# A decoder block with top-2 experts: the routing joined to the gating's program, with other prefix sums and 16-bit one-hot products

## What is computed

```python
def _L0_ffn_ref(x, gate_w, expert_w):                     # x = ln(x), 8 experts, 1024 x 1024 each
    gate_logits = jnp.einsum('bsh,he->bse', x, gate_w)
    top_vals, top_idx = jax.lax.top_k(gate_logits, 2)
    probs = jax.nn.softmax(top_vals, axis=-1)
    w_e = jnp.einsum('bsk,bske->bse', probs, jax.nn.one_hot(top_idx, 8))
    expert_out = jnp.einsum('bsh,eho->bseo', x, expert_w)
    return jnp.einsum('bseo,bse->bso', expert_out, w_e)
```

## Time and profile before

| what | us |
|---|---|
| median of 3 runs | 1199.26 |
| lowest and highest | 1190.36, 1199.87 |
| the profiled execution | 1194.41 |
| its span in the trace | 1192.4 |
| PE, DVE, POOL, ACT busy in it | 1042.3, 570.3, 487.3, 393.8 |

### The profile page before, as it was taken

How to read it: one execution, slowest core, us unless ns; L and a number is a source line. 1 busy time by engine, 2 the same in 40 slices (tenths; PEclk the granted TensorE clock), 3 DMA queues, 4 the chain that set the end, 5 groups by cost and what they waited for, 6 DMA issues and landing times. The chain is left out here.

```text
span 1192.4 us, 13599 instructions
## 1 busy us (share of the span) xinstructions
PE 1042.3 (87%) x3593; PEld 575.2 (48%) x3594; DVE 570.3 (48%) x1637; ACT 393.8 (33%) x1124; POOL 487.3 (41%) x661
## 2 busy tenths in 40 slices
PE   6786888888888869989965699999999999999995
PEld 6784454454544435425965344444444444444442
DVE  5636479788888677996965211111111111211111
ACT  2435778676756316866830000000000000000000
POOL 3834467546655201005710643333444333334431
PEclk9878899888889979988765799999999999999998
DMA  8310110110000123000795247354645636374432
GB/s 304 121 54 0 46 68 13 54 36 1 1 1 1 70 79 134 1 1 18 283 350 215 73 86 226 74 177 104 211 79 136 169 73 211 70 211 82 86 78 36
DMA packets 38462, 120.27 MB, mean 101 GB/s; under 512 B 6219, under 2 KB 9350, under 8 KB 38406
## 3 DMA queue, kind: packets, MB, share of 16 engines
q1 hardware_dynamic: 25590, 79.77, 18.1%
q0 software_dynamic: 12816, 39.86, 15.4%
HBM read 82.91 MB, written 36.70 MB: 100 GB/s over the span
## 5 line engine op out<-in xcount | busy, mean ns | idle before, releaser
L1952 PE MATMUL bank<-T,X 128*128 x1184 | 510.6, 594 | 13.9 <-DVE X L1990 10.8
L1952 PEld LDWEIGHTS bank<-T,X 128*128 128x128 f32 x1184 | 225.2, 191 | 298.6 <-issue 298.6
L2004 DVE TENSOR_SCALAR X<-bank,col_p 128x512 f32<-128x512 f32 x37 | 27.8, 750 | 410.5 <-PE bank L1952 410.5
L1970 ACT ACTIVATE X<-bank,col_p 128x512 f32<-128x512 f32 x37 | 25.4, 687 | 523.2 <-PE bank L1952 523.2
L1905 POOL DMA_INDIRECT X<-x_nrm,col_s x156 | 149.5, 958 | 92.9 <-issue 46.9
L1914 POOL DMA_INDIRECT out_dram<-X,col_d x37 | 60.0, 1622 | 268.6 <-DVE X L2004 255.0
L450 POOL TENSOR_TENSOR T<-T 128x8 f32<-128x8 f32 x216 | 94.5, 437 | 16.3
L634 PE MATMUL bank<-nat,T 128*128 128x512 f32 x128 | 88.0, 840 | 12.1 <-ACT X L787 5.4
L799 ACT ACTIVATE M<-X,T 128x256 bf16<-128x256 f32 x200 | 98.5, 497 | 0.0
L459 POOL TENSOR_TENSOR rs<-ve,neg_half 128x4 f32<-128x4 f32 x36 | 38.5, 1069 | 104.7 <-DVE ve L942 104.5
L787 ACT ACTIVATE X<-bank,T 128x512 f32<-128x512 f32 x64 | 43.8, 686 | 70.1 <-PE bank L634 69.6
(11 more groups left out here) (317 smaller groups left out, 1462.9 us busy)
## 6 DMA issues: line engine op xcount, KB each, us to landing
T<-in_L_ffn_expert_w_dram SPq DMA_DIRECT2D x8, 4096.0 KB, 17.6
out_dram<-X SPq DMA_DIRECT2D x17, 512.0 KB, 4.7
M<-in_x_dram SPq DMA_DIRECT2D x16, 512.0 KB, 7.3
X<-in_x_dram SPq DMA_DIRECT2D x16, 512.0 KB, 4.7
x_nrm<-H SPq DMA_DIRECT2D x16, 512.0 KB, 3.7
T<-in_ctx_dram SPq DMA_DIRECT2D x9, 512.0 KB, 4.0
X<-x_nrm,col_s POOLq DMA_INDIRECT x156, 3.6
X<-in_ctx_dram SPq DMA_DIRECT2D x4, 512.0 KB, 7.0
```

The lines of the kernel that those rows point to most:

```text
L1952: mm = nc.tensor.matmul(bank[2 * u + n][:, :], xgt[u][:, k, :], Tf[:, ds(odd * (KD * D) + (k * D + n * BANK), BANK)], start=(k == 0), stop ...
```

## The change

The routing's block is gone: its instructions stand at the end of the gating's block, and its small tiles are declared ahead of it. In the routing the prefix sums over tiles come from one scan by DVE on the choices themselves, and PE adds the column sums and a triangle with -1 at and below the diagonal in PSUM, so that several small DVE steps fall away. The one-hot lanes and slots are bf16: a token's number is split into two parts that bf16 holds exactly, and a weight into three pieces. The products of the weights, and what says which slot has which expert, are moved behind the first `sources` of the experts' block, beside the gathers. Expert 0 is loaded in the middle of the gating. The second part of tile 12 goes ahead of the last `back`, batch 0 takes its statistics ahead of `first_sums`, and the last steps of the logits change order. Row numbers count from 1, which costs one more row of `x_nrm`, and T's two halves for the weights are interleaved.

```diff
@@ gating, SP @@
+                    if b == B // 2:
+                        sp.wait_ge(back_mm, 2 * B)
+                        sp.wait_ge(l_mm, NT // 2)
+                        sp.dma_start(wslot[:, 0, :, :], expert_src(0)).then_inc(w_in_sem[0], 16)
                 sp.dma_start(out[N:N + P, :], X[:, 0, :]).then_inc(out_init, 16)
+                sp.dma_start(x_nrm[0:1, :], nring[0][0:1, :]).then_inc(out_init, 16)
                 sp.wait_ge(back_mm, 4 * B)
-                sp.wait_ge(l_mm, B)
-                for w in range(2):
-                    sp.dma_start(wslot[:, w, :, :], expert_src(w)).then_inc(w_in_sem[w], 16)
+                sp.wait_ge(l_mm, NT)
+                sp.dma_start(wslot[:, 1, :, :], expert_src(1)).then_inc(w_in_sem[1], 16)
@@ gating, PE @@
+                    upto = CT * b if b < B - 2 else CT * b + 1 if b < B - 1 else CT * B
+                    for t in range(done, upto):
+                        second_part(t)
...
+                pe.wait_ge(r_dve, 14)
+                nc.tensor.matmul(bank[TOTAL][:, 0:E], ones[:, :], prefix[:, :, NT - 1], start=True, stop=True).then_inc(r_pe, 1)
+                nc.tensor.matmul(bank[PLACE][:, 0:NT * E], upto_neg[:, :], flat(either), start=True, stop=False)
+                nc.tensor.matmul(bank[PLACE][:, 0:NT * E], ones[:, :], flat(prefix), start=False, stop=True).then_inc(r_pe, 1)
+                for k in range(2):
+                    pe.wait_ge(hot_set, k + 1)
+                    for t in range(NT):
+                        mm = nc.tensor.matmul(bank[TOKEN][:, 0:2 * WIDE], hot_lane[k][:, t, :], of_token[k][:, t, :, :]...)
+                for c in range(QK):
+                    for j in range(2):
+                        mm = nc.tensor.matmul(bank[SOURCE][...], sel[:, c, :], tok_parts[:, j, 0:SLOTS], ...)
@@ gating, ACT @@
+                for k in range(QK):
+                    a.copy(sel[:, k, :]..., ident[:, k * QP:(k + 1) * QP]...).then_inc(r_sel, 1)
+                a.copy(lane_row, iota_lane[:, :]).then_inc(r_sel, 1)
+                a.activation(tile_base, step_t[:, 0, :]..., ACT.Copy, scale=float(QK)).then_inc(r_sel, 1)
                 for h in range(CT):
                     normed((B - 1) * CT + h)
+                act.wait_ge(r_dve, 13)
+                a.activation(e2[:, :], e2[:, :], ACT.Exp).then_inc(r_act, 1)
@@ gating, DVE @@
                 for b in range(B):
                     residual(b)
+                    if b > 0:
+                        behind(b - 1)
+                    stats(b)
                     if b == 0:
                         first_sums(2)
                         first_sums(3)
-                    else:
-                        behind(b - 1)
-                    stats(b)
...
-                behind(B - 1)
+                dve.wait_ge(l_mm, NT)
+                then(v.tensor_tensor(known, known, bank[P2_BANK]..., ALU.add))
                 then(v.tensor_tensor(shift, over_e(mean_all(1)), over_t(g_all), ALU.mult))
                 then(v.tensor_tensor(known, known, shift, ALU.subtract))
-                dve.wait_ge(l_mm, B)
-                then(v.tensor_tensor(known, known, bank[P2_BANK]..., ALU.add))
+                behind(B - 1)
                 then(v.tensor_tensor(logits[:, :, :], known, over_e(rs_all(1)), ALU.mult))
...
+                route(v.tensor_tensor_scan(prefix..., later_t[:, :], either..., 0.0, ALU.mult, ALU.add))
+                dve.wait_ge(r_pe, 1)
+                route(v.tensor_tensor(full, step_t, bank[TOTAL]..., ALU.is_lt))
+                route(v.tensor_reduce(need, full, AX.X, ALU.add))
+                route(v.tensor_tensor_scan(end, ones[:, 0:E], need, 0.0, ALU.mult, ALU.add))
+                dve.wait_ge(r_pe, 2)
+                route(v.scalar_tensor_tensor(place, begin..., float(P), bank[PLACE]..., ALU.mult, ALU.add))
+                route(v.tensor_tensor(hot[:, :, :, :], hot[:, :, :, :], place..., ALU.mult))
+                route(v.tensor_reduce(pos_i[:, :, :], hot[:, :, :, :], AX.X, ALU.add))
+                v.tensor_scalar(lane_i, pos_i, P - 1, None, ALU.bitwise_and)
+                route(v.tensor_scalar(slot_i, pos_i, 7, None, ALU.logical_shift_right))
+                dve.wait_ge(r_sel, QK + 2)
+                v.tensor_copy(lane[:, :, :], lane_i[:, :, :])
+                for k in range(2):
+                    route(v.tensor_tensor(at_slot[k]..., iota_slot..., slot_i[:, k, :]..., ALU.is_equal))
+                    v.tensor_scalar(of_token[k][:, :, 0, 0:SLOTS], at_slot[k]..., tok1[:, 0:1], float(QK), ALU.mult, ALU.mult)
+                    v.tensor_tensor(of_token[k][:, :, 1, 0:SLOTS], at_slot[k]..., tile_base..., ALU.mult)
+                    for t in range(NT):
+                        ins = v.tensor_scalar(hot_lane[k][:, t, :], lane_row, lane[:, k, t:t + 1], None, ALU.is_equal)
+                    ins.then_inc(hot_set, 1)
+                dve.wait_ge(r_act, 1)
...
+                weigh(dve, v.tensor_copy(piece[0], prob[:, :, :]))
+                weigh(dve, v.tensor_tensor(prob_rest[0], prob[:, :, :], piece[0], ALU.subtract))
...
+                dve.wait_ge(r_pe, 3)
+                v.tensor_copy(tok_parts..., bank[TOKEN]...).then_inc(tok_set, 1)
+                for j in range(2):
+                    weighted(0, j)
+                dve.wait_ge(r_pe, 4)
+                route(v.tensor_scalar(src_i..., bank[SOURCE]..., quarter[:, 0:1], None, ALU.add))
@@ experts, SP @@
+                sp.wait_ge(cols_set, IN_FLIGHT)
@@ experts, POOL @@
-                pool.wait_ge(out_init, NT * 16 + 16)
+                pool.wait_ge(out_init, NT * 16 + 32)
@@ experts, PE, ahead of the first products @@
+                for k in range(2):
+                    pe.wait_ge(p_set, k + 1)
+                    for t in range(NT):
+                        mm = nc.tensor.matmul(bank[PROB][:, 0:3 * WIDE], hot_lane[k][:, t, :], of_prob[k][:, t, :, :]...)
+                mm.then_inc(p_mm, 1)
@@ experts, DVE @@
                 for u in range(IN_FLIGHT):
                     sources(u, u)
-                    columns(u, u)
+                weighted(0, 2).then_inc(p_set, 1)
+                v.tensor_scalar(end_i[:, :], end, 1.0, None, ALU.add)
+                weigh(dve, v.tensor_tensor(past, iota_slot..., end..., ALU.is_ge))
...
+                for j in range(3):
+                    ins = weighted(1, j)
+                ins.then_inc(p_set, 1)
+                turned(0, 0, 0)
+                sources(IN_FLIGHT, 0)
...
+                dve.wait_ge(p_mm, 1)
+                weigh(dve, v.tensor_reduce(pair_p[:, :], bank[PROB]..., AX.X, ALU.add))
+                for u in range(IN_FLIGHT):
+                    columns(u, u)
```

More of the change, by code:

```diff
@@ new lines, in decoder_kernel @@
+        best = small(2, NT)
+        hot = small(2, NT, E)
+        eq = small(NT, E)
+        first = small(NT)
+        masked = small(NT, E)
+        either = small(E, NT)
+        e2 = small(NT)
+        prob = small(2, NT)
+        prefix = small(E, NT)
+        full = small(E, NT)
+        need = small(E)
+        ends = small(E + 1)
+        begin, end = ends[:, 0:E], ends[:, 1:E + 1]
+        place = small(NT, E)
+        pos_i = small(2, NT, dt=I32)
+        lane_i = small(2, NT, dt=I32)
@@ new lines, in decoder_kernel @@
+        lane_row = small16(P)
+        tile_base = small16(NT, WIDE)
+        sel = small16(QK, QK * QP)
+        hot_lane = [natf[:, k * N:k * N + NT * P // 2].bitcast(BF16).rearrange("p (t l) -> p t l", t=NT) for k in range(2)]
+        at_slot = [small16(NT, WIDE) for _ in range(2)]
+        of_token = [small16(NT, 2, WIDE) for _ in range(2)]
+        of_prob = [small16(NT, 3, WIDE) for _ in range(2)]
+        piece = [small16(2, NT) for _ in range(3)]
+        prob_rest = [small(2, NT) for _ in range(2)]
@@ new lines, in decoder_kernel, with weigh, weighted @@
+        tok_parts = small16(2, WIDE)
+        tok4 = small(SLOTS)
+        pair_p = small(SLOTS)
+        unused = small(SLOTS)
+        src_i = small(SLOTS, QK, dt=U32)
+        p_set, p_mm, r_fin = sem("p_set"), sem("p_mm"), sem("r_fin")
+        n_weigh = [0]
+        def weigh(dve, ins):
+            n_weigh[0] += 1
+            ins.then_inc(r_fin, 1)
+            dve.wait_ge(r_fin, n_weigh[0])
+        def weighted(k, j):
+            return nc.vector.tensor_tensor(of_prob[k][:, :, j, 0:SLOTS], at_slot[k][:, :, 0:SLOTS], piece[j][:, k, :].unsqueeze(2).to_broadcast([P, NT, SLOTS]), ALU.mult)
@@ L1713, in decoder_kernel @@
-        best = small(2, NT)
-        hot = small(2, NT, E)
-        eq = small(NT, E)
-        first = small(NT)
-        masked = small(NT, E)
-        either = small(NT, E)
-        e2 = small(NT)
-        prob = small(2, NT)
-        tot = small(E, NT)
-        upto = small(E, NT)
-        full = small(E, NT)
-        need = small(E)
-        end = small(E)
-        begin = small(E)
-        place = small(NT, E)
-        pos = small(2, NT)
-        pos_i = small(2, NT, dt=I32)
-        lane_i = small(2, NT, dt=I32)
```

(26 more changed lines are left out.)

254 lines of the change are left out of this document (122 added, 132 removed).

## The result

Over 20 executions each, the changed kernel has a median of 1187.97 us and the kernel before one of 1199.37 on the same chip. Two of the changed kernel's 20 took 1400.27 and 1563.72 us, at a mean granted clock of 0.715 and 0.633 for 0.90 in the others, and the ratio leaves them out. It is 0.9924, with a 95% interval of 0.9905 to 0.9943: 0.8% faster, some 9 us by the means (11 by the medians). I had forecast 23 less and a range that ended at 1184.

The account below looks back on a forecast made before the run. What can move lies ahead of the experts' fixed PE-busy stage: 4.95 (boundary) + 1.3 (gating) + 17.0 (routing) + 0.3 (sources) - 0.5 (first gather) = 23 us less than a base of 1197, so 1174 us; range 1164 to 1184.

Parts of the forecast that it names:

- What binds: Experts' stage fixed at 513.8 us; every microsecond taken ahead of it, from gating to first gathers, ends up in the time.
- The gating: Stage up to the logits: ready 1.3 us earlier, at 613.9; bounds from a 0.8 us loss to 3 us gained.
- (a): Gating: batch 0's statistics fill DVE's 2.71 us wait for PE, moving PE's gapless stretch to the logits forward by 2.1 us.
- (b): Gating: second part of tile 12 ahead of the last `back`, same number of PE passes; no gain.
- (c): Gating's end: DVE's steps after the last product take 1.5 us instead of 0.72, a loss of 0.8 us.
- The boundary: Between gating and routing: without a block between, DVE goes on after the logits; all 4.95 us go.
- The routing: From the logits to `src_i`: 18.1 us for 35.15, 17.0 less; bounds 15.5 to 25.5 us.
- The tail: Routing's end, behind PE's token products up to `src_i`: 2.2 us, where now it is 3.7.
- Behind the boundary: Start of experts: sources done 0.3 us earlier; moved DVE and PE work hidden beside the gathers, 1.3 us of cover left.
- The rival: DVE's four two-source products beside descriptor writing delay the first gather by up to 3.2 us: 1177 us; chance 0.14.
- ACT and DMA: Early expert 0 load delays stores, still done before the gathers ask; expert 1's load can cost the first gather 0.5 us.
- the rival of the choked queue: Early expert load delays the stores the gathers wait for: 1180 us at 250 GB/s, 1199 at worst; chance 0.07.

Follow-up runs that it names:

- the run with one compare: Changed kernel with batch 0's statistics behind the first sums again and each choice's sixteen compares made in one instruction: 1178.3 us, ratio 0.9845 to the kernel before.
- the change with the wait: Changed kernel with PE waiting for three quarters of batch 3's residual, not one, ahead of batch 4's turning back: 1176.9 us, ratio 0.9839 (first job 1178.6).
- the longer one: Changed kernel with PE waiting for all four quarters of batch 3's residual ahead of batch 4's turning back: 1180.8 and 1185.2 us, ratio 0.9891.

## Why the prediction was wrong, point by point

**What binds** held: the experts' stage kept its length, and what was gained ahead came through. The base of 1197 was a choice between two values; the mean of the kernel before over its 20 executions is 1197.2, their median 1199.4, so the miss isn't there.

**The gating is the step that failed.** Its part (a) had DVE's lead move PE's stretch "forward by 2.1 us" at the length it had. It moved by 1.24 (31.00 for 32.24 us), since DVE lost 1.8 us of the 2.7 again: two shifts of 128 x 1, 0.68 us at that place before, took 2.46 beside POOL's product, and the next two gave 0.3 back. That alone is a small error. The large one is the length: I moved the stretch as it stood, with 168 ns for each of its last 64 passes, as if that were the price of a pass, when it was the price at the clock that this kernel happened to get. At 1.2 GHz the 160 passes of 8 columns and the 64 of 128 make 47.50 us, at the mixture 35.09. The windows that I had read said 0.78 for that stretch and 0.50 for what came after; my bound for the loss was 0.8 us, and nothing in the range stood for the clock going from one to the other, 12.4 us. The runs that alter only the order or a wait put it on this: 79.2 to 80.2 us where PE's run begins 31.0 us in, 68.9 or 69.0 where it begins 32.1 to 32.2 us in.

**(b)** Tile 12: nothing, as forecast. **(c)** The two steps more behind the last product: with batch 0's statistics put back, gating is 68.98 for 68.05, 0.9 more; forecast 0.8.

**The boundary**: 4.95 to 0.04, as forecast.

**The routing**: 20.1 us for a forecast 18.1; the forecasts of its parts stand in brackets below. Its rows, one choice and the products:

```profile
641.44 2.69 DVE L1855 TENSOR_SCALAR nat<-M 128x128 bf16<-128x128 bf16 x16
644.04 0.81 DVE L1850 TENSOR_TENSOR M<-iota_slot,M 128x624 bf16<-128x624 f32 x1
...
648.34 1.25 PE L1584 MATMUL bank<-M,nat 128*128 128x80 bf16 x16 [2.90 <-DVE nat L1855]
...
650.00 0.24 DVE L1868 CAST M<-bank 128x78 bf16<-128x78 f32 x1
...
651.59 0.48 DVE L1872 TENSOR_SCALAR M<-bank,quarter 128x156 uint32<-128x156 f32 x1
```

The places took 7.9 us (7.7). A choice took 4.1 and 4.2 (3.1): sixteen compares are 2.69 us, 168 ns each, where I took 90, so the row of one instruction with 128 columns was nearer than the starts of instructions with one. One compare of 2048 columns is 2.28. The Trainium skill's warning in "VectorE: DVE Perf Modes", section "The TRN2 errata — SBUF-src ops pay a fixed extra latency per instruction", has the direction right. Its formula, 94 ns for such a compare (an estimate from that page), is too little, as the section itself says of this formula for single instructions; the measurement, 168 ns, decides. PE's passes were quicker, 78 ns (120), so that DVE's eight steps of the weights were late in their stead, as foreseen: 1.7 us for 2.0. The tail: 2.1 (2.2).

**Behind the boundary**: 10.7 for a forecast 10.4. The work of DVE and PE beside the gathers was hidden: DVE still waited 3.27 us. POOL's first and third gather took longer, 1.37 and 1.31 us for 1.25 and 0.95, so that four gathers need 5.5 us from first to last, 5.0 before. The rival had up to 3.2 us for this. Two of the prediction's own signs failed here: a first gather of 1.25 us at most, and under 2 us of DVE's wait.

```profile
653.95 1.37 POOL L1916 DMA_INDIRECT X<-x_nrm,col_s  x1 [28.57 <-DVE col_s L2012]
...
656.90 1.31 POOL L1916 DMA_INDIRECT X<-x_nrm,col_s  x1 [0.30 <-issue]
...
661.38 1.25 DVE L2007 STREAM_TRANSPOSE X<-X 128x1024 f32<-128x1024 f32 x1 [3.27 <-DMA X<-x_nrm,col_s]
```

Whether DVE's two-source products cause it wasn't tried.

**ACT and DMA.** POOL was released by a source and not by a store, as forecast; the rival of the choked queue fell. In the changed kernel the early load doesn't delay the last store: that of tile 15 went out 82.3 us after the gating's start with it, and as late in the run without it (I had some 74; 68.2 before). It was late with the logits. With batch 0's statistics put back the stores do lag. DVE had the shift of tile 12 ready at 613.1, and ACT, which started 0.3 us behind such a shift elsewhere, got its place in the ring only at 622.6, some 9 us later, for want of a store that stands behind the load of expert 0. Its rows, the last one the store of tile 15, 79.5 us after the gating's start:

```profile
612.85 0.22 DVE L1771 SCALAR_TENSOR_TENSOR late<-late 128x1 f32<-128x1 f32 x2
...
622.59 1.24 ACT L1647 ACTIVATE H<-X,late 128x1024 f32<-128x1024 f32 x1 [11.93 <-DMA x_nrm<-H]
...
631.40 0.32 SPq L1459 DMA_DIRECT2D x_nrm<-H  x1
```

Expert 1's load goes out behind that store, at 633.5, and is in flight until about 648, beside the first gathers (from 642.9). With the clock put right the slack is all but used up, as the run with one compare shows.

The account of the 23 us: of 118.31 the change with the wait takes 99.77, 18.5 less. The routing lacks 2.0 us of the forecast, the gating 2.1 (a gain of 1.3 that is a loss of 0.8), the start 0.4. The change as it stands gives back 11.2 more through the clock. With the wait the kernel takes 1176.9 us, inside the range that was forecast: without the loss of the clock the range would have held.

## What to carry to other kernels

Where PE works without a gap at a granted clock between 0.5 and 1, the price of a pass isn't a constant: read the clock of each stretch, work out its length at both levels, and put both into the range, above all where an edit moves when the stretch begins. A reordering that fills another engine's wait should be timed alone, because it can cost much of what the rest of a change gains: here 11 of 18.4 us. And a store queue that a large load is put into should be followed to its last store and to the load behind it: here that is what took back the next 0.8 us.

## What the runs showed of the hardware that was not expected

A wait of 1.1 us more on PE made 224 passes 12.4 us shorter. In the profiles with and without the shorter wait the 16 passes of batch 4's turning back run at 1.2 GHz (3.65 to 3.68 us); where they begin 32.1 or 32.2 us after the gating's start, the 32 passes behind them run at 2.4, and where they begin 31.0 us after it, no pass does for 47.5 us. The moment of the rise doesn't follow the start of the run. The rise that the changed kernel lacks comes 35.9 us after the gating's start in the kernel before, with the shorter wait and with the longer one alike, though their runs begin 32.24, 32.11 and 32.72 us in. These are the windows from that moment up to where the clock falls again, in the three and, at the same place, in the changed kernel:

```profile
583.05:586.45 3.40, 3.40 (x33) 3.40 (x32) 3.22 (x7) 3.40 (x7) 1.82 (x3) 1.00 0.94 372
587.65:591.05 3.40, 3.40 (x32) 3.40 (x33) 3.33 (x7) 3.26 (x7) 2.58 (x2) 1.00 1.02 410
583.57:586.97 3.40, 3.40 (x33) 3.40 (x32) 3.32 (x7) 3.28 (x7) 2.56 (x2) 1.00 0.86 347
587.68:591.08 3.40, 3.40 (x18) 3.40 (x17) 3.34 (x7) 3.25 (x7) 2.59 (x2) 0.50 0.85 336
```

What PE had been at by then differs. In the three its passes of 128 columns had just ended or were ending (the passes of 8 columns begin 35.7, 35.6 and 36.0 us in); in the changed kernel it had been at passes of 8 columns since 34.4. That this is what kept the clock low is a reading of these rows; no run changes it by itself. The Trainium skill's "TensorE: Matmul & The Clock Gate", section "Part 1: The HAM clock gate (the "warmup" mystery)", says that PE starts throttled and that activity lifts this. The runs agree as far as that four added products a tile raised the clock from 0.50 to 0.79; but two behind each of the last eight tiles went with a fall from 0.69 to 0.63.

The clock also has a part in the levels that the executions fall into. In the 14 profiles, of whatever kernel, the gating starts at 542.5 to 542.7, 546.9 to 547.7 or 551.8 to 553.0 us. Between the two profiles of before and after, 4.6 us appear at one place in code that the change doesn't touch; PE's rows of the kernel before and of the changed one there:

```profile
177.81 3.95 PE L634 MATMUL bank<-nat,T 128*128 128x512 f32 x8
```

```profile
180.57 5.83 PE L634 MATMUL bank<-nat,T 128*128 128x512 f32 x8
```

The second starts 2.8 us later than the first and takes 1.9 longer. The clock of 165 to 200 us is 0.90 in the one and 0.78 in the other, and from there on they run 4.6 us apart, almost to the hundredth, for 350 us. One execution against one is therefore uncertain by 5 us, and by 10 between the outer levels, on this kernel.
